# Which engine makes the low half of the attention probabilities: an even split between GpSimd and VectorE, or three to one

## What is computed

```python
xn = jax.nn.silu(group_norm(x, gn_scale, gn_offset))
qkv = jnp.einsum('bxyc,cd->bxyd', xn, w_qkv)
q, k, v = jnp.split(qkv, 3, axis=-1)
q, k, v = (to_heads(q), to_heads(k), to_heads(v))
q = q * HEAD_CH ** (-0.5)
sim = jnp.einsum('bhdi,bhdj->bhij', q, k)
attn = jax.nn.softmax(sim, axis=-1)
out = jnp.einsum('bhij,bhdj->bhid', attn, v)
out = jnp.einsum('bxyd,dc->bxyc', out, w_out) + b_out
return out + x
```

## Time and profile before

| | us |
|---|---|
| median of 3 runs | 4288.79 |
| lowest and highest run | 4285.77, 4290.7 |
| profiled execution: span | 4293.1 |

### The profile page before, as it was taken

One profiled execution on the slowest core, in us unless ns is written; L12 is line 12 of the kernel. 1 busy time (PEld: TensorE's weight loads), 2 busy tenths in 40 slices (PEclk: granted clock), 3 DMA queues, 4 the chain that ended last, 5 costly groups with the idle time before them and its releaser, 6 DMA issues.

```text
span 4293.1 us, 94034 instructions
## 1 busy us (share of the span) xinstructions
PE 4020.1 (94%) x32844; PEld 2046.2 (48%) x32844; DVE 3129.0 (73%) x5216; ACT 2837.5 (66%) x3202; POOL 1627.1 (38%) x1226
## 2 busy tenths in 40 slices
PE   3999999899999999999999999999999999999997
PEld 1444545444454444445445454444544444444443
DVE  5687777767777677776777777677776777768774
ACT  2576676667667676676766766676676776767664
POOL 1243343433334333343433434334343333434333
PEclk8999999999999999999999999999999999999999
DMA  2111212122031120311212121220311203111121
GB/s 76 30 46 48 60 29 75 31 60 61 16 90 31 50 56 18 88 31 53 53 34 72 31 74 32 54 66 16 85 36 48 58 16 90 31 53 53 31 63 36
DMA packets 119497, 212.44 MB, mean 49 GB/s; under 512 B 19536, under 2 KB 19536, under 8 KB 118992
## 3 DMA queue, kind: packets, MB, share of 16 engines
q1 hardware_dynamic: 118992, 205.86, 17.8%
HBM read 71.57 MB, written 33.55 MB: 24 GB/s over the span
## 4 chain that ended last, share of the span: by engine, by line
PE 66%; issue 17%; POOL 7%; DVE 6%; ACT 3%; DVEq 0%; POOLq 0%; DMA 0%; SPq 0%; ACTq 0%
PE SD L929 29%; PE PV L1052 12%; PE TP L943 9%; PE ST L1018 6%; PE ST L1019 6%; POOL Pl L492 5%; DVE Pl L795 2%; DVE mx L741 2%; PE SD L992 1%; POOL xn L479 1%; PE TP L951 1%; ACT QK_hi L553 1%; PE SD L986 1%; ACT Ph L594 1%; ACT V L558 1%
## 5 line engine op out<-in xcount | busy, mean ns | idle before, releaser
L741 DVE TENSOR_REDUCE mx<-TP 128x1 f32<-128x512 f32 x2048 | 1349.9, 683 | 412.1 <-PE TP L943 403.2
L591 ACT ACTIVATE P<-ST,cns 128x1024 f32<-128x1024 f32 x1024 | 1143.6, 1117 | 598.4 <-PE ST L1019 551.0
L492 POOL TENSOR_TENSOR Pl<-P,Ph 128x1024 f16<-128x1024 f32 x512 | 1117.1, 2182 | 795.2 <-ACT Ph L594 795.1
L594 ACT ACTIVATE Ph<-ST,cns 128x1024 f16<-128x1024 f32 x1024 | 1138.8, 1112 | 0.0
L1052 PE MATMUL PV<-V,Ph 128*128 128x129 f16 (+2 forms) x10240 | 888.7, 213 | 34.8 <-POOL Pl L492 22.0
L1052 PEld LDWEIGHTS PV<-V,Ph 128*128 128x128 f16 x10240 | 769.5, 98 | 303.6 <-issue 268.9
L1052 PE MATMUL PV<-V,Pl 128*128 128x65 f16 x8192 | 853.8, 194 | 0.0
L1018 PE MATMUL ST<-Q,K 128*128 128x512 f16 x2048 | 796.4, 389 | 48.9 <-issue 48.9
L1019 PE MATMUL ST<-Q,K 128*128 128x512 f16 x2048 | 796.3, 389 | 0.0
L943 PE MATMUL TP<-QK_hi 64*128 64x512 f16 x2048 | 729.6, 392 | 61.2 <-DVE mx L741 42.0
L929 PE MATMUL SD<-xn,wq 128*128 128x512 f16 x3072 | 733.7, 381 | 25.2 <-POOL xn L479 16.0
(11 more groups left out here) (92 smaller groups left out, 2828.9 us busy)
## 6 DMA issues: line engine op xcount, KB each, us to landing
work<-in_x SPq DMA_DIRECT2D x128, 256.0 KB, 2.8
Q<-QK_hi SPq DMA_DIRECT2D x256, 128.0 KB, 2.6
K<-QK_hi SPq DMA_DIRECT2D x256, 128.0 KB, 2.8
res<-in_x SPq DMA_DIRECT2D x128, 256.0 KB, 3.2
out<-res SPq DMA_DIRECT2D x128, 256.0 KB, 2.3
K<-QK_lo SPq DMA_DIRECT2D x128, 128.0 KB, 2.7
Q<-QK_lo SPq DMA_DIRECT2D x128, 128.0 KB, 2.6
V<-in_L_conv_w_qkv SPq DMA_DIRECT2D x1, 3072.0 KB, 10.7
```

The lines of the kernel that those rows point to most:

```text
L492: nc.gpsimd.tensor_tensor(Pl[:, v % 4, :], P32[:, v % 2, :], Ph[:, v % 4, :], ALU.subtract).then_inc(lo_pool, 1)
L591: nc.scalar.activation(P32[:, v % 2, :], ST[:, v % 2, :], ACT.Exp, scale=cns[:, 0:1])
L594: nc.scalar.activation(Ph[:, v % 4, :], ST[:, v % 2, :], ACT.Exp, scale=cns[:, 0:1]).then_inc(exp_done, 1)
L741: nc.vector.reduce_max(mx[:, hh, qb, kh:kh + 1], TP[:, cnt.top_bank], AX.X).then_inc(top_drained, 1)
```

## The change

`low_probs` of a unit with v % 4 == 0 stays on VectorE. Units with v % 4 == 2 move from VectorE to GpSimd, so that GpSimd makes 768 of the 1024 low halves and VectorE 256. The two semaphores and the waits on them follow (`splits_before` counts what an engine has made). Nothing else is moved.

```diff
+def splits_on_dve(v):
+    return v % 4 == 0
+
+def splits_before(b, v):
+    return 16 * b + v // 4 if splits_on_dve(v) else 48 * b + 3 * (v // 4) + v % 4 - 1
...
@@ gpsimd, step
-                    if v % 2 == 0 and not (first and v == 0):
+                    if not splits_on_dve(v - 1) and not (first and v == 0):
                         low_probs(b, v - 1)
@@ scalar, exponentials
-                if v % 2 == 0:
-                    wait(act, lo_dve, 32 * b + v // 2)
+                if splits_on_dve(v - 2):
+                    wait(act, lo_dve, splits_before(b, v - 2) + 1)
                 else:
-                    wait(act, lo_pool, 32 * b + v // 2)
+                    wait(act, lo_pool, splits_before(b, v - 2) + 1)
@@ vector, step
-                    if v % 2 == 1:
+                    if splits_on_dve(v - 1):
                         low_probs(b, v - 1)
@@ tensor, times_v
-                    if v % 2 == 0:
-                        pe.wait_ge(lo_dve, 32 * b + v // 2 + 1)
+                    if splits_on_dve(v):
+                        pe.wait_ge(lo_dve, splits_before(b, v) + 1)
                     else:
-                        pe.wait_ge(lo_pool, 32 * b + v // 2 + 1)
+                        pe.wait_ge(lo_pool, splits_before(b, v) + 1)
```

## The result

The changed kernel takes 4350.78 us (median of 4 runs, 4348.45 to 4353.52) against 4289.74 us of the kernel before; the ratio is 1.0146, 95% interval 1.0131 to 1.0160. That is +61 us where +33 us was forecast, inside the stated range and on its slow side.

What follows compares the result with a forecast made beforehand. TensorE, busy 94%, was taken as the bound, so only its waits count. Costs of +3.85 us and gains of -1.65 gave +2.2 us per image, times 15 +33 us: 4289 + 33 = 4322 us, range 4278 to 4362.

Steps and rivals of the forecast that it cites:

- TensorE's clock: At 2.7, the longer wait brings another stretch at 1.2 GHz, costing 25 us: 4347 us; chance 0.15.
- caught twice: At 2.6, L780 is also held, by GpSimd's subtraction of 2.7, another 31 us: 4353 us; chance 0.12.
- The hold at 2.6: Largest term: L774 held by GpSimd's subtraction of 2.6, delaying `QK_lo` and TensorE's product: +1.9 us per image.
- The sign of being wrong: In the changed profile, TensorE's granted clock changing by more than 0.003 would show the prediction wrong.
- The late places of step 2: GpSimd's moved subtractions end later: +0.95 us at 2.15, +0.5 at 2.11, +0.3 at 2.2, per image.
- The gains: TensorE's waits at 3.4 and 3.12 go (1.0 + 0.4 us), 0.25 of 0.59 at 0.8: -1.65 us per image.
- Faster: L774 at 2.6 starts before GpSimd, and the slow-clock stretch near 2.11 halves: 4268 us; chance 0.15.
- slips through: At 2.6, L774 gets in before GpSimd's subtraction, nothing else changes: +0.3 us per image, 4293 us; chance 0.12.

Runs made afterwards that it cites:

- The three moved units: Kernel before with only units 0.6, 3.2 and 3.10 of each image moved to GpSimd: 4265.04 us, ratio 0.9941.
- The short delay: Kernel before plus one unused VectorE reduction over 820 numbers per image at 2.6, taking 1.00 us: 4299.99 us, ratio 1.0020.
- twice the delay: Kernel before plus one unused VectorE reduction over 1780 numbers per image at 2.6, taking 2.00 us: 4349.02 us, ratio 1.0138.

## Why the prediction was right, and where it was short

The direction and the largest term were right for the reason given. The size was not: +61 us is nearly twice the +33 us forecast, and the measured time stands where the forecast had put its rivals "TensorE's clock" (4347 us) and "caught twice" (4353 us), of which the first came about. That it lies in the range is due to the room that the range left for the rivals.

**The hold at 2.6 (+1.9 us forecast).** Right as it was worked out. L774's successor took 2.05 us, GpSimd's second subtraction followed the first at once, and the wait grew from 0.26 to 2.18 us, by 1.92. That holds in 14 of the 15 images; in the last, L783 alone is held, where before neither was, and the wait is 2.18 us too. The chain was caught once and not twice: L791 began at 2130.49 and the subtraction of 2.7 at 2130.64, so the margin was 0.15 us. The forecast had 0.09 us for it: this came out as said, but by little.

**The clock.** Here the step failed that put the half-speed stretch among the rivals at 0.15 instead of into the sum. In the changed kernel a half-speed stretch began behind this wait in 12 of the 15 images that have the chain, and the reason given against it, that ScalarE and VectorE would hide TensorE's slowness, did not hold: in the stretch's 3.40 us VectorE was busy for 0.48 us and ScalarE for 0.86 us (the second row of the stretches above), and the product ran 1.7 us longer (4.45 against 2.76 us) with scores, exponentials and reductions behind it. The rival's own price, 15 x 1.7 = 25 us, was close for the stretches behind the wait (12 x 1.7 = 20 us) and had nothing for the others in step 2. The forecast had 33 us of waits and nothing for the clock; by the division above the waits came to 23 us and the clock to 36. The sign of being wrong that the prediction had named, a granted clock that changes by more than 0.003, came: it changed by 0.008. The forecast also took the timing of an image to repeat within tens of ns. For the length of the held operation that is so; the half-speed stretches do not repeat, since at the start of step 2 they last 3.4 to 10.2 us in the kernel before, from one image to the next.

**The late places of step 2.** The product of 2.14 waits 0.81 us (0.95 forecast) and that of 2.9, which the kernel before also makes wait, 1.04 us:

```profile
2172.16 0.23 PE L1063 MATMUL PV<-V,Ph 128*128 128x129 f16 x1 [0.81 <-POOL Pl L503]
```

For 2.10 and 2.14 the sum had left out that L785 of the kernel before (L796 now) could be held. It is, in every image:

```profile
2151.64 2.20 DVE L796 SCALAR_TENSOR_TENSOR work<-work 128x512 f32<-128x512 f32 x1
...
2170.65 2.00 DVE L796 SCALAR_TENSOR_TENSOR work<-work 128x512 f32<-128x512 f32 x1
```

2.2 and 2.0 us where it takes 0.68. In the kernel before only one of its 128 took over 0.8 us, before the loop. So the rule in the Trainium skill (SBUF — State Buffer, section Who interferes with whom) on operations with two SBUF inputs holds in the trace, also for this kind of operation. The three units 2.2, 2.10 and 2.14 cost 2.1 us per image by the runs, 1.75 were forecast; the 2.1 has a part of the clock in it that the 1.75 had not. No experiment takes the three apart.

**The gains (-1.65 us forecast).** The waits at 3.4 (0.90 us) and 3.12 (0.29 us) are gone, and so is the 0.59 us at 0.8, of which 0.25 had been counted: the copy L821 now begins 0.73 us ahead of GpSimd's next subtraction and lengthens it to 2.54 us, not to 3.39.

```profile
2265.65 1.28 DVE L821 COPY V<-V 128x4160 f16<-128x4160 f16 x1
...
2266.38 2.54 POOL L503 TENSOR_TENSOR Pl<-P,Ph 128x1024 f16<-128x1024 f32 x1 [0.55 <-ACT Ph L605]
```

The three moved units give 26 us in 16 images, 1.6 us per image, and the mean clock stays (0.974 against 0.973).

**The rivals.** "Faster" and "slips through" failed at the point that they named: the second subtraction was there before the next small operation. "Caught twice" did not happen in the changed kernel; its mechanism showed when the chain was placed 2 us later.

## What to carry to other kernels

Before work is moved from VectorE to GpSimd, look at what VectorE does between SBUF tiles while GpSimd would be running: a chain of tiny dependent operations pays one whole GpSimd operation for each time it must get past one, and two GpSimd operations back to back catch it twice. An even ratio between two engines is the wrong unit of choice; here 3 places of 16 made most of the gain, one made 55 to 65 us of loss and three others 34 us, and the order of each place could be read from the timeline. A wait of TensorE is not worth its length alone: price what the clock does behind it as well, from places in the same trace, and take the clock of the whole step and not of this place alone.

## What the runs showed of the hardware that was not expected

- When GpSimd has its next operation ready, a small VectorE operation that was held gets through and the one behind it does not: L783 ended at 2127.95, GpSimd's second subtraction had begun at 2127.89, L785 began at 2127.99 and was held for 2.05 us.
- The float16 copy is not held like the others: in the earlier trace rows it began 0.18 us after GpSimd's subtraction, took its usual 1.23 us, and GpSimd's operation grew by 1.26 us instead. The Trainium skill (SBUF — State Buffer, section Who interferes with whom) gives the pair to whoever starts first for the whole operation; this copy started second and was not held, and here the rows decide. L785 began only 0.10 us behind its GpSimd operation and was held, so it is not simply that 0.18 us is too short for GpSimd to be under way. Why the copy fares otherwise, no run shows.
- A wait of TensorE of 2.15 us, with GpSimd's work as it was, was followed by a half-speed stretch of 3.4 us in 9 of 15 images, one of 1.14 us in none. In the changed kernel 12 of 15 waits of 2.18 us were. The short delay also made the clock better elsewhere in step 2, which no run explains; with both, twice the delay cost 58 us instead of 9 us. In the kernel before, another place has a half-speed stretch behind waits of 0.52 and 1.63 us close to each other, ahead of the 6.8 us of the earlier trace rows:

```profile
2110.89 0.23 PE L1052 MATMUL PV<-V,Ph 128*128 128x129 f16 x1 [0.52 <-DVE Pl L795]
2113.71 0.39 PE L943 MATMUL TP<-QK_hi 64*128 64x512 f16 x1 [1.63 <-DVE mx L741]
```
